# A transformer block on one core: two step tables of the feed-forwards rewritten, so that other work stands beside VectorE's maxima

## What is computed

```python
# shapes: x (8, 512, 128), H = 16 heads, HD = 8
x = x + 0.5 * ffn(layernorm(x))        # "f1"
x = x + attention(layernorm(x))        # "pj" is its projection part
x = x + 0.5 * ffn(layernorm(x))        # "f2"

def ffn(x):
    return quant(x, delta_act) @ quant(weight, delta_w).T + bias

def quant(x, delta):                   # per block of 32
    amax = max(abs(x));  e = floor(log2(amax))
    scale = exp2(e - 2) * exp2(0.5 * tanh(4 * delta))
    xs = x / scale
    return scale * sign(xs) * round_to_fp4(min(abs(xs), 6))

def attention(x):
    q, k, v = rope(x @ wq.T + bq), rope(x @ wk.T + bk), x @ wv.T + bv
    return softmax(q @ k.T / sqrt(HD)) @ v
```

## Time and profile before

| what | value |
|---|---|
| runs (3): median, lowest, highest | 566.05, 565.73, 569.64 us |
| profiled execution: its own time | 568.19 us |
| its span, first to last instruction | 566.4 us |
| TensorE, VectorE, ScalarE, GpSimd busy | 486.6, 441.3, 396.8, 229.8 us |
| mean granted TensorE clock | 0.947 of full speed |

### The profile page before, as it was taken

One profiled execution on the slowest core, in us unless ns is written; L12 is line 12 of the kernel. 1 busy time (PEld: TensorE's weight loads), 2 busy tenths in 40 slices (PEclk: granted clock), 3 DMA queues, 4 the chain that ended last, 5 costly groups with the idle time before them and its releaser, 6 DMA issues.

```text
span 566.4 us, 10225 instructions
## 1 busy us (share of the span) xinstructions
PE 486.6 (86%) x2662; PEld 171.0 (30%) x2662; DVE 441.3 (78%) x1020; ACT 396.8 (70%) x766; POOL 229.8 (41%) x350
## 2 busy tenths in 40 slices
PE   0453899999999999999999989999899999998851
PEld 0221232333233323433333323333233323322211
DVE  6656999877998689868797688869897689888125
ACT  4745278687968787878667677878767787677840
POOL 8000185226552655346552555346552544002310
PEclk9995599999999999999799989999899999999995
DMA  2313202310123012301222012301222023200000
GB/s 71 113 27 108 89 11 65 97 58 12 48 85 104 9 49 86 103 4 38 65 77 70 12 47 85 103 1 29 71 78 67 12 59 94 84 1 2 21 0 19
DMA packets 26047, 30.82 MB, mean 54 GB/s; under 512 B 6150, under 2 KB 21388, under 8 KB 25996
## 3 DMA queue, kind: packets, MB, share of 16 engines
q1 hardware_dynamic: 24364, 29.87, 17.7%
q10 hardware_dynamic: 1632, 0.39, 0.3%
HBM read 21.47 MB, written 8.39 MB: 53 GB/s over the span
## 4 chain that ended last, share of the span: by engine, by line
PE 64%; DVE 17%; issue 8%; ACT 5%; POOL 4%; DVEq 1%; POOLq 0%; ACTq 0%
PE ot L1112 18%; PE sc L1099 16%; PE st L1088 13%; DVE negmax L885 6%; PE misc L1052 4%; PE misc L1077 3%; PE misc L1035 3%; ACT probs L636 2%; ACT feat_k L527 2%; DVE amax_f L777 2%; PE misc L1060 1%; DVE stats_f L753 1%; PE misc L1030 1%; PE misc L1069 1%; PE sc L1052 1%
## 5 line engine op out<-in xcount | busy, mean ns | idle before, releaser
L885 DVE TENSOR_REDUCE negmax<-sc 128x1 f32<-128x512 f32 x512 | 333.0, 683 | 70.1 <-PE sc L1099 67.0
L636 ACT ACTIVATE probs<-st 128x512 f32<-128x512 f32 x512 | 272.9, 601 | 77.1 <-PE st L1088 74.1
L1099 PE MATMUL sc<-feat_k,feat_q 96*128 96x512 bf16 x512 | 190.9, 398 | 12.2 <-DVE negmax L885 11.7
L1088 PE MATMUL st<-feat_q,feat_k 99*128 99x512 bf16 x512 | 159.0, 385 | 6.6 <-ACT probs L636 5.6
L1112 PE MATMUL ot<-probs,vfeat 128*32 128x512 f32 x1024 | 138.3, 613 | 1.0 <-ACT probs L636 1.0
L1099 PEld LDWEIGHTS sc<-feat_k,feat_q 96*128 96x128 bf16 x512 | 50.0, 98 | 168.0 <-DVE negmax L885 122.6
L1088 PEld LDWEIGHTS st<-feat_q,feat_k 99*128 99x128 bf16 x512 | 49.9, 99 | 79.7 <-ACT probs L636 47.6
L462 POOL TENSOR_TENSOR qkpre<-qkpre,ropeT 128x512 f32<-128x512 f32 x28 | 35.4, 1272 | 40.1 <-ACT qkpre L585 40.1
L447 POOL TENSOR_SCALAR maxparts<-negmax 128x16 bf16<-128x16 f32 x32 | 8.3, 259 | 71.3 <-DVE negmax L885 71.3
L486 POOL TENSOR_TENSOR xres<-xres,onorm 128x128 f32 (+1 forms) x31 | 14.1, 454 | 54.6 <-DVE onorm L902 54.6
L1052 PE MATMUL misc<-xnT,wqkT 128*128 128x512 f32 x56 | 30.4, 625 | 2.0 <-DVE onorm L902 2.0
(11 more groups left out here) (132 smaller groups left out, 465.4 us busy)
## 6 DMA issues: line engine op xcount, KB each, us to landing
feat_q<-parts_q SPq DMA_DIRECT2D x96, 96.0 KB
feat_k<-parts_k SPq DMA_DIRECT2D x96, 96.0 KB
parts_q<-qkparts_q SPq DMA_DIRECT2D x24, 128.0 KB, 2.4
parts_k<-qkparts_k SPq DMA_DIRECT2D x24, 128.0 KB, 2.3
xres<-in_L_attn_x_dram SPq DMA_DIRECT2D x8, 256.0 KB, 5.0
out_dram<-xres SPq DMA_DIRECT2D x8, 256.0 KB, 2.5
feat_q<-maxrows ACTq DMA_DIRECT2D x32, 12.0 KB
wload<-in_L_ffn_weight_dram SPq DMA_DIRECT2D x1, 64.0 KB, 2.5
```

What stands on the lines that cost most here:

```text
L636: nc.scalar.activation(probs[:, s % US, j * S:(j + 1) * S], st[:, bank(2 * s + j), :], ACT.Exp, scale=SCALE).then_inc(exp_done, 1)
L885: nc.vector.tensor_reduce(negmax[:, g, j:j + 1], sc[:, bank(16 * g + j), :], AX.X, ALU.max, negate=True).then_inc(sc_maxed, 1)
L1088: nc.tensor.matmul(st[:, bank(2 * s + j), :], feat["k"][par][0:MROWS, h, kb * P:(kb + 1) * P], feat["q"][par][0:MROWS, h, :], start=True, ...
L1099: nc.tensor.matmul(sc[:, bank(16 * g + j), :], feat["q"][par][0:SROWS, h, t * P:(t + 1) * P], feat["k"][par][0:SROWS, h, :], start=True, s ...
```

## The change

Six numbers of FFN1, six of FFN2 and two of PROJ change. The table before stays in force for the first feed-forward of batch 1 (`FIRST`), which `turns` sees to; every use of `turns_of_batch` with a table becomes one of `turns`. No operation is added or removed.

```diff
-FFN1 = dict(stats=3, rstd=4, norm=6, amax=8, scale=10, expo=11, quant=11, turn=15, mul=16)
-PROJ = dict(stats=20, rstd=21, norm=23, turn=25, qk=(27, 29, 31, 32), rope=(28, 30, 33, 34), high=(32, 37),
+FFN1 = dict(stats=1, rstd=2, norm=3, amax=5, scale=10, expo=11, quant=11, turn=14, mul=15)
+PROJ = dict(stats=21, rstd=22, norm=23, turn=25, qk=(27, 29, 31, 32), rope=(28, 30, 33, 34), high=(32, 37),
             rest=(35, 38), mid=(36, 39), low=(38, 40), write=40, load=(44, 52), v=35)
-FFN2 = dict(stats=7, rstd=9, norm=11, amax=13, scale=16, expo=16, quant=19, turn=22, mul=23, store=29)
+FFN2 = dict(stats=7, rstd=9, norm=11, amax=14, scale=17, expo=18, quant=20, turn=23, mul=24, store=29)
+FIRST = {("f1", 1): dict(FFN1, stats=3, rstd=4, norm=6, amax=8, turn=15, mul=16)}
...
+        def turns(b, par, s, n, key, first, i=None, later=0):
+
+            table = dict(f1=FFN1, f2=FFN2, pj=PROJ)[n]
+            step = (table[key] if i is None else table[key][i]) + later
+            out = [(nb, npar) for nb, npar in turns_of_batch(b, par, s, step, first) if not known(nb) or (n, nb) not in FIRST]
+            for (name, nb), own in FIRST.items():
+                if known(b) and name == n:
+                    step = (own[key] if i is None else own[key][i]) + later
+                    out += [turn for turn in turns_of_batch(b, par, s, step, first) if turn[0] == nb]
+            return out
```

More of the change, by code:

```diff
@@ L495, in slot @@
                             attended(nb, g)
-                    for n, at, first in (("f2", FFN2, -1), ("f1", FFN1, 2), ("pj", PROJ, 2)):
-                        for nb, _ in turns_of_batch(b, par, s, at["rstd"], first):
+                    for n, first in (("f2", -1), ("f1", 2), ("pj", 2)):
+                        for nb, _ in turns(b, par, s, n, "rstd", first):
                             rstd(n, nb)
@@ L649, in slot @@
                         copy_out(nb, g)
-                    for n, at, first in (("f2", FFN2, -1), ("f1", FFN1, 2), ("pj", PROJ, 2)):
+                    for n, first in (("f2", -1), ("f1", 2), ("pj", 2)):
                         for half in range(2):
-                            for nb, _ in turns_of_batch(b, par, s, at["norm"] + half, first):
+                            for nb, _ in turns(b, par, s, n, "norm", first, later=half):
                                 if not hurried(n, nb):
@@ L659, in slot @@
                         feature_rows("k", 1, 1)
-                    for n, at, first in (("f2", FFN2, -1), ("f1", FFN1, 2)):
-                        for nb, _ in turns_of_batch(b, par, s, at["turn"], first):
+                    for n, first in (("f2", -1), ("f1", 2)):
+                        for nb, _ in turns(b, par, s, n, "turn", first):
                             copy_xqT(n, nb)
@@ L665, in slot @@
                                 feature_rows("k", 0, 1)
-                    for nb, _ in turns_of_batch(b, par, s, PROJ["turn"], 2):
+                    for nb, _ in turns(b, par, s, "pj", "turn", 2):
                         copy_xnT(nb)
@@ L919, in slot @@
                         invert_sums(nb, g)
-                    for n, at, first in (("f2", FFN2, -1), ("f1", FFN1, 2)):
-                        for nb, _ in turns_of_batch(b, par, s, at["mul"] + 1, first):
+                    for n, first in (("f2", -1), ("f1", 2)):
+                        for nb, _ in turns(b, par, s, n, "mul", first, later=1):
                             add_ffn(n, nb)
@@ L957, in slot @@
                                 exponents(n, nb, 2)
-                        for nb, _ in turns_of_batch(b, par, s, at["expo"] + 1, first):
+                        for nb, _ in turns(b, par, s, n, "expo", first, later=1):
                             if not hurried(n, nb):
                                 exponents(n, nb, 2)
-                        for nb, _ in turns_of_batch(b, par, s, at["quant"], first):
+                        for nb, _ in turns(b, par, s, n, "quant", first):
                             if hurried(n, nb):
```

68 lines of the change are left out of this document (34 added, 34 removed).

## The result

| what | before | after |
|---|---|---|
| runs, median (lowest to highest) | 567.85 us (565.73 to 571.17, 4 runs) | 608.38 us (604.58 to 612.78, 4 runs) |
| profiled execution, its span | 568.19, 566.4 us | 610.36, 608.3 us |
| mean granted TensorE clock | 0.947 | 0.924 |

The changed kernel is slower: its time is 1.079 of the kernel before, 95% interval 1.073 to 1.084. The sign of the forecast (580.4 us) holds and its size does not; the time lies beyond the top of the range, 595.

What follows compares the result with a forecast made beforehand. TensorE was taken to set the pace, with other engines interrupting it. From 566.05 us, relief -5.5, step 6 +6.3, f1's transposes +5.1, f2's copy +10.0 and clock -1.6 gave 580.4 us; range 568 to 595.

Steps and rivals of the forecast that it cites:

- The three new waits: TensorE waits at f1's transposes (GpSimd or VectorE), f2's product (ScalarE's copy), and step 6 (late exponentials); +5.1, +10.0, +6.3 us.
- The relief: Steps 7 to 11: moving f1's block scales to steps 5 to 7 shortens TensorE's stretch; -5.5 us, bounds -8 and -1.
- Steps 1 to 6: Step 6: f1's early deviation delays GpSimd's second rotation, then the exponentials; 1.05 us per slot, +6.3 us, bounds 2 and 8.
- Steps 22 to 25: f2's product waits 2.0 us for ScalarE's copy, behind the projections' norm, in five slots; +10.0 us, bounds 6 and 11.5.
- The transposes of f1: Steps 13 to 17: turned one step earlier, they wait 2.15 us for quant; net 0.85 in six slots, +5.1 us.
- steps 17 to 21: Moved f2 and projection pieces on VectorE costed at nothing, covered by its slack; otherwise 0.3 us in a slot.
- The clock: Three old half-clock falls go (6.0 us), two new ones come (+4.4); -1.6 us, bounds -6 and +11.
- the clock falls at most of the 2 us waits: Rival, slower still: eight new half-clock falls instead of two, giving 593.6 us; chance 0.20.

Runs made afterwards that it cites:

- f: Changed kernel with ScalarE's copy of the values ahead of the norm, and GpSimd's rotations ahead of the inverse deviations: 607.58 us, ratio 1.079.
- b: Changed kernel with turn and product of f1 put back to steps 15 and 16: 585.44 us, ratio 1.034.
- d: Changed kernel with two unread products on TensorE ahead of its wait for f1's quantisation, batches 2 and up: 592.90 us, ratio 1.046.
- j: Changed kernel with ScalarE's copy of the transposed quantised input ahead of the norms: 589.83 us, ratio 1.035.
- g: Changed kernel with f1's four small block-scale operations moved to steps 8 to 10, the reduction left in step 5: 593.67 us, ratio 1.055.
- m: Kernel before with f1's norm at step 5, f2's stats at 9, expo at 18, and f2's rstd, norm, amax, scale, quant one step later: 567.31 us, ratio 1.007.
- n: m with f2's inverse deviation at step 11 instead of 10, behind f1's scaled values on GpSimd: 561.09 us, ratio 0.994.

## Why the prediction was wrong

**The sign and most of the places were right.** The three new waits that I named are there, with the releasers that I gave: the transposes of f1 for GpSimd, the product of f2 for ScalarE's copy, step 6 for the exponentials. The relief is not there, and part of the wait of step 6 stands in step 4.

**Steps 1 to 6, +6.3.** Measured +7.1, of which one fall in slot 4 is 1.6; so 5.5 of waiting. I put all of it in step 6; it is split between the transposes of step 4 (behind ScalarE's `copy_v`, which I did not trace) and step 6. The size is near, the cause only in part mine: by f the rotation queued behind the deviation is 0.3 to 0.4 us of 0.9 to 1.0 in four slots, and the larger part is ScalarE's norm of f1, which I had counted only as using up idle time.

**Steps 22 to 25, +10.0.** The wait is 1.96 us by b and d, where I had 2.0. In five slots and with 0.95 in slot 0, it is 10.7. The term is right in size, and j shows its cause for 1.1 to 1.4 us of the 1.96.

**The transposes of f1, +5.1.** Mis-sized. I had a wait of 2.15 us (measured idle time 1.7 to 2.0 us in steps 14 and 15 of a slot), and counted 1.35 of it as given back by VectorE catching up, which leaves 0.80 a slot; my sum used 0.85. Without the clock it is 7.4 in all (d): against b, 1.0 to 1.1 in each of slots 1 to 5 and 1.9 in slot 0, so much less was given back. And steps 17 to 21, which I called covered, cost 2.6 more, of which 0.9 is the clock in slot 0; the other 1.7 is 0.33 in each of five slots. The size is the 0.3 that I had named, but not its cause: b took it away with the turn.

**The relief of steps 7 to 11, -5.5.** This step failed. Measured +1.3 in steps 7 to 10, outside its own bounds of -8 and -1. I had the mechanism in the text and gave it too little weight: that small operations of VectorE wait for GpSimd's, with a bound of -1. Two of them do in every slot and a third in four, and the g rows show them at a quarter to a half of the length when they don't. The sum that I made (7.2 us from step 7 to 11) is what m and n measured, 7.19; there the small operations stand behind the last maximum of step 8, where the first still meets GpSimd (0.90 us in step 9) and holds up no maximum of that unit. The old loss was also a little smaller than my 14.5, namely 13.8, since slot 0 has no f2 and took 7.19.

**The clock, -1.6.** This step failed the most, by 16.2 us, and lies beyond its own upper bound of +11. The old falls did go (-7.0 in steps 11 to 13, forecast -6.0). But I took two new falls from one observation, that a slot losing 1.92 us in pieces had none. There were twelve, and by d, b and the step lengths they cost 1.6 + 12.2 + 7.8 = 21.6 us (one in steps 1 to 6, where step 3 of slot 4 took 4.92 us instead of 3.28; six at the turn, 11.3 in steps 14 to 16 and 0.9 behind; five at the copy, at about 1.57). The loss before was in pieces; here TensorE stood for one piece of 1.0 to 2.0 us, in most slots with another short wait ahead of it, like the 1.34 of the earlier trace rows, which did have a fall. That is not the whole condition, as the same waits had none in most slots of b, d and g. My rival "the clock falls at most of the 2 us waits" was the case that happened, and even it had eight falls for twelve.

Together, with all that is clock counted apart: -0.8 in steps 1 to 6, +6.8 relief, +2.3 turn, +1.7 steps 17 to 21, +0.7 copy, and +16.2 for the clock, which is +14.6 (21.6 less 7.0) instead of -1.6. That is 26.9 of the 27.0 us between forecast (14.3) and profile (41.3).

## What to carry to other kernels

A piece of work moved to a quieter place on one engine must be followed through every other queue it stands in: here numbers in a table set a norm before a copy on ScalarE and a deviation before a rotation on GpSimd, and TensorE got a wait from each in nearly every slot. A wait of TensorE of one to two us in one piece should be priced with the half-clock stretch that may follow it, unless the trace shows that such waits go unpunished; here the clock, less the old falls, was a third of the loss. And before small VectorE operations are spread out, look at what GpSimd does in the steps where they go.
